# First listed job step's weights fetched whole, and 2 and 4 filling products for 4 and 11 around layer 0's last combination

## What is computed

```
x = x + attention0(layernorm(x))          # relative positions in layer 0
t = layernorm(x)
for e in range(8):                        # layer 0: gated experts, 432 to 1584 wide
    w = sum(where(top2_index == e, top2_value, 0))
    h = (silu(t @ gate[e].T) * (t @ up[e].T)) @ down[e].T
    out = out + w * h
x = x + t + out
x = x + attention1(layernorm(x))
t = layernorm(x)
for e in range(8):                        # layer 1: 768 wide, relu, with biases
    out = out + w[e] * (relu(t @ w1[e].T + b1[e]) @ w2[e].T + b2[e])
x = x + t + out
```

## Time and profile before

| | |
|---|---|
| median of 3 runs | 205.91 us (204.89 to 206.14) |
| the profiled execution's own time | 206.71 us |
| its span, first to last instruction | 204.9 us |
| mean granted TensorE clock | 0.982 of full speed |
| moved by DMA | 50.05 MB, mean 244 GB/s |

### The profile page before, as it was taken

How to read it: one execution, slowest core, us unless ns; L and a number is a source line. 1 busy time by engine, 2 the same in 40 slices (tenths; PEclk the granted TensorE clock), 3 DMA queues, 4 the chain that set the end, 5 groups by cost and what they waited for, 6 DMA issues and landing times.

```text
span 204.9 us, 4386 instructions
## 1 busy us (share of the span) xinstructions
PE 186.7 (91%) x1656; PEld 130.3 (64%) x1656; DVE 99.7 (49%) x300; ACT 63.3 (31%) x144; POOL 32.1 (16%) x65
## 2 busy tenths in 40 slices
PE   7899899989999999999999698899999999993992
PEld 7779777658546656675558577565685667571571
DVE  0433696847852222454322219876478685440131
ACT  2234477834412222131124216876241000000000
POOL 1314400001495000000000104000007900000000
PEclk9999999999999999999999999999999999997599
DMA  6999999994400018899800999994000589999001
GB/s 203 435 402 439 419 434 416 430 409 168 156 0 3 0 33 309 317 419 419 353 7 0 304 400 419 418 428 201 0 3 0 148 285 326 392 277 329 22 3 43
DMA packets 9693, 50.05 MB, mean 244 GB/s; under 512 B 1400, under 2 KB 2880, under 8 KB 7488
## 3 DMA queue, kind: packets, MB, share of 16 engines
q1 hardware_dynamic: 9088, 48.89, 62.4%
q10 hardware_dynamic: 576, 0.79, 1.3%
HBM read 49.48 MB, written 0.20 MB: 242 GB/s over the span
## 4 chain that ended last, share of the span: by engine, by line
PE 63%; issue 10%; DVE 8%; DMA 7%; SPq 6%; ACT 3%; POOL 1%; DVEq 0%; ACTq 0%; POOLq 0%
PE bank L1394 6%; PE bank L1102 5%; PE bank L1476 5%; PE bank L1220 5%; DMA w<-bias_rows_dram 5%; PE bank L1175 4%; PE bank L1421 4%; PE bank L1350 4%; PE bank L1461 3%; PE bank L1378 3%; PE bank L1232 3%; PE bank L1434 3%; PE bank L1204 3%; DMA x<-x_dram 2%; SPq L501 2%
## 5 line engine op out<-in xcount | busy, mean ns | idle before, releaser
L1102 PE MATMUL bank<-ones 128*128 128x128 f32 x162 | 23.7, 300 | 2.0 <-POOL ones L539 1.4
L1102 PEld LDWEIGHTS bank<-ones 128*128 128x128 f32 x162 | 21.8, 211 | 2.8 <-POOL ones L539 1.4
L698 ACT ACTIVATE scratch<-bank,neg_max 128x256 f32<-128x256 f32 x48 | 19.7, 479 | 7.8 <-DVE neg_max L823 7.6
L1394 PE MATMUL bank<-w,scratch 128*64 128x512 f32 (+3 forms) x112 | 20.4, 490 | 0.3 <-ACT scratch L723 0.3
L1476 PE MATMUL bank<-w,scratch 128*64 128x192 f32 x216 | 20.2, 332 | 0.0
L1476 PEld LDWEIGHTS bank<-w,scratch 128*64 128x64 f32 x216 | 14.4, 136 | 9.1 <-issue 5.7
L589 POOL TENSOR_SCALAR scratch<-const,place,gate 128x64 f32<-128x64 f32 x32 | 18.1, 582 | 5.8 <-issue 5.8
L547 POOL TENSOR_TENSOR rstd<-var_eps,minus_half 128x2 f32<-128x2 f32 x4 | 2.8, 710 | 98.0 <-DVE var_eps L760 98.0
L1220 PE MATMUL bank<-const,scratch 128*128 128x128 f32 x96 | 15.1, 284 | 2.5 <-ACT scratch L698 1.2
L823 DVE TENSOR_REDUCE neg_max<-bank 128x2 f32<-128x512 f32 x24 | 15.7, 682 | 3.2 <-PE bank L1204 3.2
L1015 DVE TENSOR_TENSOR scratch<-scratch,bank 128x512 f32<-128x512 f32 (+1 forms) x10 | 6.6, 661 | 19.2 <-ACT scratch L634 19.2
(11 more groups left out here) (178 smaller groups left out, 280.5 us busy)
## 6 DMA issues: line engine op xcount, KB each, us to landing
w<-experts_dram SPq DMA_DIRECT2D x8, 1152.0 KB, 18.0
w<-experts_dram SPq DMA_DIRECT2D x14, 576.0 KB, 8.2
w<-items_dram SPq DMA_DIRECT2D x8, 768.0 KB, 6.8
w<-experts_dram SPq DMA_DIRECT2D x1, 3624.0 KB, 13.6
w<-items_dram SPq DMA_DIRECT2D x8, 384.0 KB, 7.1
w<-experts_dram SPq DMA_DIRECT2D x1, 3024.0 KB, 30.9
w<-experts_dram SPq DMA_DIRECT2D x1, 2496.0 KB, 20.0
w<-experts_dram SPq DMA_DIRECT2D x1, 2016.0 KB, 24.3
```

The lines of the kernel that those rows point to most:

```text
L698: nc.scalar.activation(probs[:, h % HB, t, :], bank[h % HB][:, t * TOK:(t + 1) * TOK], ACT.Exp, bias=neg_max[:, h, t:t + 1]).then_inc(prob ...
L1102: nc.tensor.matmul(bank[b][:, 0:P], ones[:], ones[:], start=True, stop=True)
L1394: nc.tensor.matmul(first_bank(m, which)[rows, to:to + wide], xe_hi[:, e], w0[:, at:at + wide], start=col == 0, stop=False, tile_position=( ...
```

## The change

Two edits. The first: in both layers, the units of the first listed step (k = 0) are fetched whole, with one transfer each that counts up `job_landed`; its four down transfers and TensorE's wait for `job_down_landed[layer][0]` are gone. Later steps keep their two transfers. The second: 2 filling products for 4 ahead of layer 0's last combination, 4 for 11 behind it. They are written into every case of the tree.

```diff
-KEEP_START, KEEP_SCORES, KEEP_FIRST, KEEP_ROUTE, KEEP_PLACE, KEEP_SUM, KEEP_NORM = 16, 6, (4, 6), 7, 4, 4, 11
+KEEP_START, KEEP_SCORES, KEEP_FIRST, KEEP_ROUTE, KEEP_PLACE, KEEP_SUM, KEEP_NORM = 16, 6, (4, 6), 7, 4, 2, 4
...
+                            front = ROOM if k == 0 else DOWN_AT[layer]
                             with sp.If(more > QUADS * k + q + 1):
-                                sp.dma_start(w0[:, at:at + DOWN_AT[layer]], wholes[q][:, 0:DOWN_AT[layer]]).then_inc(job_landed[layer][k], 16)
+                                sp.dma_start(w0[:, at:at + front], wholes[q][:, 0:front]).then_inc(job_landed[layer][k], 16)
...
-                        for q in range(QUADS):
+                        for q in range(QUADS if k > 0 else 0):
                             at = ROOMS[layer][k % 2][q][0] + DOWN_AT[layer]
...
                     pe.wait_ge(sems["y_ready"], sums_before_job(layer, k))
-                    pe.wait_ge(job_down_landed[layer][k], QUADS * 16)
+                    if k > 0:
+                        pe.wait_ge(job_down_landed[layer][k], QUADS * 16)
```

## The result

| | before | changed |
|---|---|---|
| median of 4 runs, us | 205.78 (204.89 to 206.14) | 207.78 (207.64 to 207.95) |
| profiled execution: time, span | 206.71, 204.9 | 207.64, 205.6 |
| mean granted TensorE clock | 0.982 | 0.971 |

What follows compares the result with a forecast made beforehand. The prediction took TensorE's waits and low clock as the bound: 206.71 - 0.6 (jump) - 0.7 (layer 1 fetch) = 205.4 us, less 0.8 for the median, gave 204.6. The range was 202.7 to 207.3.

Steps and rivals of the forecast that it cites:

- What bounds the kernel: TensorE, busy 186.7 of 204.9 us; time winnable at layer 0's expert end and layer 1's second step, including low clock.
- The filling products, combination: Ahead of layer 0's last combination, halving the filling products moves the combination and the engines behind it 0.54 us sooner.
- The filling products, the jump: Leaving layer 0's job cases, fewer filling products bring the jump, and so layer 1's first transposes, sooner; gain 0.6 us.
- My bounds, 0 to 1.16: Limits on the jump's gain: nothing if its instruction fetch does not move, at most 1.16 us, capped by x.
- The whole fetch, layer 0: Layer 0's whole units land before TensorE asks for them; cost and gain nothing.
- The whole fetch, layer 1: Layer 1's second step lands at 187.2 instead of 187.9; gain 0.7 us, bounds nothing to 3.3.
- Only the gaps close: Layer 1's earlier issues only fill idle DMA shares of 0.72 and 0.93 in 164 to 168, worth 0.7 us.
- Waits 0.4: Layer 1's first step now waits for its down parts, 0.4 us (up to 1.1), costing nothing at the end.
- the short wait keeps the clock: Rival, layer 1's second step: 2.1 us of idle leaves the clock high, winning 2.7 us more, 202.7; chance 0.30.
- the clock falls behind the drain: Rival, after layer 0's experts: longer idle drops TensorE to 1.2 GHz, costing 2.7 us, 207.3; chance 0.25.
- The whole unit late: Rival, layer 1's first step: its whole units land at 180.8, the step starts 3.1 us later, 205.2; chance 0.10.
- nothing moves: Rival: neither jump nor landings bind, 0.54 us or less is won, 205.4 to 205.9; chance 0.05.

Runs made afterwards that it cites:

- after_moved: The changed kernel plus 44 never-executed filling products that move the jump's target to 81 instructions ahead of its packet's end; 201.42 us, ratio 0.9837.
- fill_moved: The kernel before with only the new filling products (2 and 4), plus 44 never-executed ones placing the jump's target 81 instructions ahead; 205.0 us, ratio 0.9928.
- nine_fill: The changed kernel with 2 and 9 filling products, plus 48 never-executed ones placing the jump's target 81 instructions ahead; 200.32 us, ratio 0.9772.
- late_again: The changed kernel with SP's layer 1 expert loads held back until TensorE's first transposes there, rerun beside the changed kernel; 204.88 us against 208.14.
- fill_only: The kernel before with only the new filling products (2 and 4), fetches as before; 210.5 us, ratio 1.0238.

## Why the prediction was wrong

**What bounds the kernel** was read rightly: both places, the late jump and the wait with its low clock, are where the time moved.

**The filling products, combination.** Right: "the whole 0.54 counts"; 0.45 of it are seen. The combination starts 110.35 - 108.23 = 2.12 us behind the start of the down products, before 110.85 - 108.28 = 2.57. At the scaled x 0.34 are left (6.00 against 6.34 us), since the combination itself took 0.77 for 0.67.

**The filling products, the jump: the step that failed.** I wrote "What does is that the jump comes sooner" and "Gain 0.6", and took the jump as the last thing between x and the transposes. The jump did come sooner, by 1.6 us and not 0.6:

```profile
L434 PEldq COMPARE_BRANCH  x1: 3417/3417/3417, 111.8 to 111.8; - x1
```

before, and in the changed kernel:

```profile
L434 PEldq COMPARE_BRANCH  x1: 3297/3297/3297, 110.2 to 110.2; - x1
```

But what was removed was also code, 36 instructions in each of twelve cases: the step asked when the jump is executed and never where it lands. With the target at the end of its packet TensorE has to wait for a second one, behind SP's loads. That cost 120.18 - 115.39 = 4.8 us, and 1.1 net on top (5.88 - 4.8): the low clock costs 1.7 at L1135 alone, and 0.9 comes back since VectorE is no longer late (see the last section). My bounds, 0 to 1.16, held no loss at all, though an instruction packet stood in the earlier trace rows (it begins at 112.78 and takes 1.00 us; I read the window as its length) and the loads stood in the same stretch of the trace. With the target moved back the mechanism is right and the term too small: the transposes start 6.15 us behind the start of the down products in after_moved (114.10 - 107.95) and 6.14 in fill_moved (114.46 - 108.32), against 7.11 before, so 0.96 for my 0.6. The jump is over before x is ready, and x alone sets them. In the medians this is 0.7 (fill_moved) and 1.9 (within the whole fetch), with the clock's part in both.

The Trainium skill, Runtime: NRT & Kernel Launch, section Instruction fetch mechanics, which the prediction drew on for the jump, also says that instructions come in blocks of 256 and that crossing into the next is mostly hidden. The traces agree on the 256 and not on the hiding: behind a jump, with the target at the end of its block, the crossing cost 5.95 us here, and 2.96 with idle DMA engines.

**The whole fetch, layer 0.** Right: TensorE's first listed products start at 95.43 and 101.21 without a wait for a landing, as in the earlier trace rows.

**The whole fetch, layer 1: mis-sized.** "Only the gaps close ... 0.7 us" measured 1.9 on average (2.6 between the two profiled executions, of which before was the slowest of its kind). There the last bias rows are issued 13.83 us behind the first issue instead of 17.34, 3.5 sooner, and land 2.6 sooner. My sum let 0.7 of it through. The step took the gaps from the share of busy DMA engines in the earlier trace rows (0.72, 0.93), where the row's own last column had it: 270 and 292 GB/s, against the 382 that the changed kernel has over ten microseconds of the same stretch. "Waits 0.4" for the first step measured 0.28.

**The rivals.** The first, that the short wait keeps the clock (0.30, 2.7 us), came true: 0.51 us of idle, 2.61 won. It came with a wait far below the 2.1 us that it was argued from. The second, that the clock falls behind the drain (0.25), came true as well, in the changed kernel (0.50 from 115) and without the stall: after_moved has it at 1.2 GHz over 117 to 119 (window below), and 4.51 instead of 2.83 us for L1135 make 1.7, not 2.7. Its time of 207.3 stands near the measured 207.78 by chance, since it held neither the stall nor the 5.2 us won in layer 1. The whole unit late (0.10) and nothing moves (0.05) did not happen. With all forecast mechanisms at their measured sizes and without the stall the answer is after_moved's 201.42. No case of mine held that. The window:

```profile
117.00:119.00 2.00, 2.00 (x6) 1.63 (x5) 0.00 (x0) 0.00 (x0) 0.00 (x0) 0.50 1.06 430
```

## What to carry to other kernels

Taking out instructions moves all code behind them. Where a jump separates two parts of the critical path, count how many instructions stand between its target and the end of that packet, and what the DMA engines do at that time; some never executed instructions were worth 6.4 us here. To judge a change by its work, compare versions at the same placement. Read the headroom of a fetch from GB/s beside the best stretch of the same kernel, not from the busy share.

## What the hardware showed that I had not expected

- The jump out of the tree occupies TensorE's sequencer for 3.3 to 3.9 us (3297 to 3857 ns over all fifteen profiled executions), where VectorE's own at the same line takes 51 ns. It spans the fetch of its target's packet: in the changed kernel it begins at 110.2, the packet goes from 111.21 to 112.13, and it ends at 113.5. In all fifteen it ends 1.38 to 1.46 us after that packet, as TensorE goes on 1.21 to 1.43 after the second. It is hidden as long as x is what the transposes wait for.
- The sequencer runs ahead of TensorE by 17 records. With 8 or 14 filling records behind the combination the jump begins 0.05 to 0.07 us after the combination's first record, with 18 it is 0.77 and with 22 it is 1.11 to 1.12. In the five kernels with 14 or more, 17 records had not begun at that moment.
- VectorE can be late by itself too. Before, its L782 begins 1.96 us behind the start of L1149 (122.40 - 120.44), in the changed kernel 0.82, and the filling products that follow come 0.9 us later for it. nine_fill still has 1.38. The chain calls this wait "issue" as well; what it waits for is not shown.
- The clock did not fall after a fixed idle time. In late_again it still stood at 1.00 in 114.9 to 116.0 and has a mean of 0.57 in 117 to 118, so it fell near 117.1, 5.1 us after the last product (112.1); in the changed kernel it fell at 115.0, 3.0 us after; fill_moved's second listed step waited 2.73 us and kept it, fill_only's waited 2.88 and lost it. What decides it is not shown by these runs.
- A share of busy DMA engines of 0.97 stood for 299 GB/s in one order of transfers and 1.02 for 382 in another.
